# A decoder layer on one core: projections and query features in pieces between the first maxima and around the last results

## The reference

```python
x = layernorm(x + linear_attention(x))        # 16 heads of 64, features relu(q @ RF), relu(k @ RF)
x = layernorm(x + self_and_cross(x, ctx))     # 16 heads of 16: causal self-attention over 512 rows,
                                              # cross-attention over 1024 context rows; the sum goes through Wp + bp
x = layernorm(x + experts(x))                 # 8 experts, 256 -> 1024 -> 256, the best one for each row
```

## Time and profile before

| | us |
|---|---|
| median of 3 runs (2553.83 to 2562.61) | 2555.13 |
| the profiled execution's own time | 2561.64 |
| its span, first to last instruction | 2559.6 |

### The profile page before, as it was taken

How to read it: one execution, slowest core, us unless ns; L and a number is a source line. 1 busy time by engine, 2 the same in 40 slices (tenths; PEclk the granted TensorE clock), 3 DMA queues, 4 the chain that set the end, 5 groups by cost and what they waited for, 6 DMA issues and landing times. The chain is left out here.

```text
span 2559.6 us, 52199 instructions
## 1 busy us (share of the span) xinstructions
PE 2368.7 (93%) x17502; PEld 1508.8 (59%) x17503; DVE 1451.7 (57%) x3670; ACT 997.6 (39%) x1366; POOL 325.6 (13%) x510
## 2 busy tenths in 40 slices
PE   7999989999999999989999999999999999699997
PEld 4566455655565456545664556555654565388887
DVE  2588247833784458625883378347843686234444
ACT  1156313651265116621563146413652166123332
POOL 1000020002000200020000200020002000112222
PEclk9989998999799989999899979997999799899999
DMA  7430025101510061004300250015100610455543
GB/s 219 167 118 22 2 87 186 43 1 59 203 54 2 24 228 63 2 10 163 122 22 4 109 172 32 1 59 214 43 2 27 225 63 2 159 173 167 164 164 116
DMA packets 115129, 236.45 MB, mean 92 GB/s; under 512 B 18078, under 2 KB 42015, under 8 KB 112704
## 3 DMA queue, kind: packets, MB, share of 16 engines
q1 hardware_dynamic: 111472, 224.81, 25.6%
q0 software_dynamic: 3408, 8.41, 0.9%
HBM read 160.92 MB, written 73.17 MB: 91 GB/s over the span
## 5 line engine op out<-in xcount | busy, mean ns | idle before, releaser
L1040 ACT ACTIVATE es<-ps 128x1024 f32<-128x1024 f32 (+1 forms) x704 | 660.1, 983 | 352.3 <-PE ps L686 266.4
L1229 DVE TENSOR_REDUCE craw<-ps 128x1 f32<-128x512 f32 x1024 | 637.7, 684 | 102.9 <-PE ps L651 92.0
L651 PE MATMUL ps<-hk,hq 64*128 64x512 f32 x1024 | 337.8, 528 | 27.5 <-DVE va L1213 17.7
L714 PE MATMUL ps<-es,vca 128*32 128x256 f32 x4096 | 281.2, 386 | 1.1
L651 PEld LDWEIGHTS ps<-hk,hq 64*128 64x128 f32 x1024 | 162.0, 207 | 188.5 <-DVE craw L1229 120.7
L566 POOL TENSOR_SCALAR_AFFINE_SELECT es<-es 128x256 f32<-128x256 f32 x256 | 100.0, 409 | 1215.4 <-ACT es L1040 1215.4
L1226 DVE TENSOR_REDUCE craw<-ps 128x1 f32<-128x512 f32 (+3 forms) x512 | 220.0, 485 | 60.4 <-PE ps L647 57.5
L684 PE MATMUL ps<-hq,hk 64*128 64x512 f32 x1024 | 240.9, 434 | 1.9 <-ACT es L1040 1.9
L686 PE MATMUL ps<-mrow,minus 64*128 64x512 f32 x1024 | 222.7, 400 | 0.0
L714 PEld LDWEIGHTS ps<-es,vca 128*32 128x32 f32 x4096 | 106.6, 109 | 111.7 <-issue 63.9
L1529 ACT ACTIVATE hT<-ph,b1s 128x128 f32<-128x128 f32 x312 | 89.2, 369 | 199.5 <-PE ph L1492 199.5
(11 more groups left out here) (197 smaller groups left out, 2951.2 us busy)
## 6 DMA issues: line engine op xcount, KB each, us to landing
w1s<-in_w1T SPq DMA_DIRECT2D x39, 1024.0 KB, 5.3
hk<-scr_kc SPq DMA_DIRECT2D x64, 512.0 KB, 5.1
scr_kc<-staged SPq DMA_DIRECT2D x16, 1024.0 KB, 3.8
scr_qc<-staged SPq DMA_DIRECT2D x32, 512.0 KB, 4.6
scr_q<-staged SPq DMA_DIRECT2D x32, 512.0 KB, 5.6
hq<-scr_qc SPq DMA_DIRECT2D x64, 256.0 KB, 4.8
hq<-scr_q SPq DMA_DIRECT2D x64, 256.0 KB, 4.3
hk<-scr_k SPq DMA_DIRECT2D x64, 256.0 KB, 5.2
```

The lines of the kernel that those rows point to most:

```text
L651: last = mm(pb, hq[i][at, T + t * P:T + (t + 1) * P], hk[i][at, T + half * BANK:T + (half + 1) * BANK], start=True, stop=True)
L714: last = mm(z[row:row + ZW, (2 - len(tiles)) * P:2 * P], (va if own else vca)[:, j, p * HB + a, :], weights, start=n in (0, NSELF), stop=n ...
L1040: nc.scalar.activation(es[:, k % ERING, :].rearrange("p (a c) -> p a c", a=HB)[:, :, 0:w], eslot[k % 2][:].rearrange("p (a c) -> p a c", a ...
L1229: last = v.reduce_max(craw[p % 2][:, t, a:a + 1, half], pb, AX.X)
```

## The change

- Each job names its PSUM buffer and the jobs that had it before (`SLOT`, `FORMER`), and two small jobs may share one in halves (`HALF`).
- In the first pair, behind each of five groups of three maxima, stands one piece of PE work: k1, then the halves of qf0 and qf1 (of the next batch). qf2 is cut around the last turn of results, qf3 and kf2 around the jobs at the end.
- phi_q has memory of its own; `va` and `vca` have 17 columns per head instead of 32.
- The low parts of qc1, q1 and k1 are made by POOL, from a second copy (`whole`) that ACT writes.
- The value biases are folded into bp at the start ((bv + bcv) Wp), so that ACT copies vc0, vc1 and v; kf0 and kf1 are copied by ACT too.
- Of the sums over phi_k, only the first stays on POOL; the other two are on DVE, behind the routing.
- The next x is loaded after g1, the next context after kc1. The first expert's weights are loaded at the end of the batches, and `experts` loads its rows before b2.

```diff
-VW = 2 * XD + 1
+VW = XD + 1
+JOBS = [
+    ("g0", "A", 0, ("rank",)), ("ksum", "D", 1, ("kf2",)), ("norm", "D", 2, ("gate",)), ("g1", "A", 3, ("kf3",)),
...
+    ("kc1", "B", 0, ("attn0",)), ("x1T", "A", 1, ("attn1",)), ("qc0", "B", 2, ("vc0",)), ("q0", "B", 3, ("vc1",)),
+    ("k0", "B", 0, ("kc1",)), ("v", "A", 2, ("qc0",)), ("qc1", "A", 3, ("q0",)), ("q1", "A", 3, ("q0",)),
+    ("k1", "A", 2, ("v",)), ("qf0", "A", 3, ("qc1", "q1")), ("qf1", "A", 2, ("k1",)),
+    ("qf2", "A", 2, ()), ("yT", "A", 3, ()), ("proj0", "D", 0, ()), ("proj1", "D", 0, ()), ("qf3", "A", 1, ()),
+    ("kf0", "A", 2, ("qf2",)), ("kf1", "A", 3, ("yT",)), ("x2T", "A", 0, ("proj0", "proj1")), ("gate", "D", 2, ("kf0",)),
+    ("kf2", "A", 1, ("qf3",)), ("rank", "D", 0, ("x2T",)), ("kf3", "A", 3, ("kf1",))]
...
+POOL_LOW = ("qc1", "q1", "k1")
+FIRST_PARTS = [("k1", 0), ("qf0", 0), ("qf0", 1), ("qf1", 0), ("qf1", 1)]
+PARTS = {"qf0": 2, "qf1": 2, "qf2": 2, "qf3": 2, "kf2": 2}
...
-    order = take(MAXES + AHEAD)
+    order = []
+    for name, part in FIRST_PARTS:
+        order += take(3)
+        order.append(("part", name, part))
+    order += take(MAXES + AHEAD - 3 * len(FIRST_PARTS))
...
-    return order + turns
+    return order + [("part", "qf2", 0)] + turns + [("part", "qf2", 1)]
...
+        with nc.sbuf_tensor("whole", [P, len(POOL_LOW), T], F32) as whole:
+            pass
         hk.append(sb("hk4", [P, T + TC_], F32R))
+        with nc.sbuf_tensor("big_c", [P, 4 * LR], F32) as big_c:
+            pass
+        vca = sb("vca", [P, NTC, XH, VW])
+        es = sb("es", [P, ERING, HB * BANK])
+        big_a = sb("big_a", [P, NPAIR * T])
+        with nc.sbuf_tensor("big_b", [P, NT * LR], F32) as big_b:
+            pass
+        staged = sb("staged", [P, 2, 2, 2 * T], F32R)
...
             with sp.Fori(0, nb) as b:
                 store(b, "kc0")
+                sp.wait_ge(s_xb, cur(b, 2, 1))
+                sp.sem_inc(s_pace, 1)
+                sp.wait_ge(s_tile, cur(b, NJ, JN["g1"] + 1))
+                sp.sem_inc(s_pace, 1)
+                load_x(following)
                 stored(b, ("kc0",))
...
                 store(b, "kc1")
+                sp.wait_ge(s_tile, cur(b, NJ, JN["kc1"] + 1))
+                sp.sem_inc(s_pace, 1)
+                load_context(following)
                 for n in ("qc0", "q0", "k0"):
                     store(b, n)
...
+            def part(b, name, n, fill):
+                last = fill(ready(b, name) if n == 0 else ps[SLOT[name]], (n,))
+                if n == PARTS[name] - 1:
+                    last.then_inc(s_tile, 1)
...
+                if k == 0:
+                    pe.wait_ge(s_act, cur(b, N_ACT, ACT_AT["qf1"]))
...
-                            last = mm(z[row:row + ZW, (2 - len(tiles)) * P:2 * P], (va if own else vca)[:, j, p * HB + a, :], weights,
+                            last = mm(z[row:row + VW, (2 - len(tiles)) * P:2 * P], (va if own else vca)[:, j, p * HB + a, :], weights,
...
                 job(b, "yT", turn(y_s))
+                part(b, "qf3", 0, qfeat(3))
                 job(b, "proj0", rows(yT_s, wp_s, (0, 1)), act="yT")
                 job(b, "proj1", rows(yT_s, wp_s, (2, 3)))
-                pe.wait_ge(s_x, (b + 2) * 48)
-                for i in range(NQF):
-                    job(b, f"qf{i}", qfeat(i))
+                part(b, "qf3", 1, qfeat(3))
                 job(b, "kf0", kfeat(0))
+                job(b, "kf1", kfeat(1))
                 pe.wait_ge(s_ln, cur(b, 2, 2))
                 job(b, "x2T", turn(x1))
-                job(b, "kf1", kfeat(1))
+                part(b, "kf2", 0, kfeat(2))
...
                 job(b, "gate", gate, act="x2T")
-                job(b, "kf2", kfeat(2))
+                part(b, "kf2", 1, kfeat(2))
...
+                def whole_part(name, bias_n):
+                    t = full(name)
+                    high_part(name, bias_n, 1, T, last=False)
+                    nc.scalar.activation(whole[:, POOL_LOW.index(name), :], t[:, 0:T], ACT.Identity,
+                                         bias=bias_c[:, bias_n, 1:2]).then_inc(s_act, 1)
...
+                for n, name in enumerate(POOL_LOW):
+                    stg, at, _ = STAGED[name]
+                    pool.wait_ge(s_act, cur(b, N_ACT, ACT_AT[name]))
+                    nc.gpsimd.tensor_tensor(stage[:, stg, 1, at:at + T], whole[:, n, :],
+                                            stage[:, stg, 0, at:at + T].bitcast(F32), ALU.subtract).then_inc(s_low, 1)
...
+            def other_sums(psums):
+                v.tensor_tensor(psum23, phik[:, 2, :], phik[:, 3, :], ALU.add).then_inc(s_psum, 1)
+                dve.wait_ge(s_psum, psums)
+                v.tensor_tensor(psum01, psum01, psum23, ALU.add).then_inc(s_psum, 1)
...
+            sp.wait_ge(s_dve, N_DVE * (nb + 1))
+            sp.wait_ge(s_eid, nb)
+            load_weights(sp, eid, w1s, b1s, w1T, b1p, s_w, 0, 0)
...
-            load_weights(0, 0)
             sp.wait_ge(s_moved, B * NT * 16)
             load_rows(0, 0)
+            sp.dma_start(b2s[:], b2.rearrange("e c -> (e c)").unsqueeze(0).broadcast_to([P, E * C])).then_inc(s_w2, 16)
```

More of the change, by code:

```diff
@@ L728, in qfeat, with fill @@
             def qfeat(i):
-                def fill(t):
-                    for a in range(2):
+                def fill(t, halves=(0, 1)):
+                    for a in halves:
                         j = 2 * i + a
@@ L739, in kfeat, with fill @@
             def kfeat(i):
-                def fill(t):
-                    for half in range(2):
+                def fill(t, halves=(0, 1)):
+                    for half in halves:
                         for c in range(KC):
@@ L747, in kfeat @@
                 return fill
-            pe.wait_ge(s_x, 48)
+            pe.wait_ge(s_x, 32)
             pe.wait_ge(s_setup, 3)
-            for i in range(NQF):
-                qfeat(i)(ps[JN[f"qf{i}"] % 4]).then_inc(s_tile, 1)
-            assert JN["kf0"] - JN["qf0"] == 4 and JN["kf1"] - JN["qf2"] == 4
-            assert JN["kf2"] - JN["kf0"] == 4 and JN["kf3"] - JN["kf1"] == 4
-            pe.wait_ge(s_act, ACT_AT["qf0"])
-            kfeat(0)(ps[JN["kf0"] % 4]).then_inc(s_tile, 1)
-            pe.wait_ge(s_tile, JN["kf0"] + 1)
-            pe.sem_inc(s_tile, 1)
-            pe.wait_ge(s_act, ACT_AT["qf2"])
-            kfeat(1)(ps[JN["kf1"] % 4]).then_inc(s_tile, 1)
-            pe.wait_ge(s_tile, JN["kf1"] + 1)
-            pe.sem_inc(s_tile, 1)
-            pe.wait_ge(s_dve, DVE_AT["kf0"])
-            kfeat(2)(ps[JN["kf2"] % 4]).then_inc(s_tile, 1)
-            pe.wait_ge(s_tile, JN["kf2"] + 1)
-            pe.sem_inc(s_tile, 1)
-            pe.wait_ge(s_dve, DVE_AT["kf1"])
-            kfeat(3)(ps[JN["kf3"] % 4]).then_inc(s_tile, 1)
+            for n in range(2 * NQF):
+                if n >= NQF:
+                    pe.wait_ge(s_relu, n - NQF + 1)
+                (qfeat(n) if n < NQF else kfeat(n - NQF))(ps[n % NQF]).then_inc(s_early, 1)
             pe.wait_ge(s_const, 16 * LOADS)
             pe.wait_ge(s_setup, 4)
+            pe.wait_ge(s_relu, NQF + 1)
+            pe.wait_ge(s_fold, 1)
+            for c in range(KC):
+                last = mm(ps[0][:, 0:C], bv_c[:, 0, c:c + 1].broadcast_to([P, P]), wp_s[:, c, :], start=c == 0, stop=c == KC - 1)
+            last.then_inc(s_early, 1)
+            pe.wait_ge(s_early, 2 * NQF + 1)
+            pe.sem_inc(s_tile, NJ)
             with pe.Fori(0, nb) as b:
@@ L1018, in _ @@
                                          ACT.Copy).then_inc(s_act, 1)
+                for k in range(2):
+                    t = full(f"vc{k}")
+                    nc.scalar.activation(vca[:, 4 * k:4 * k + 4, :, 0:XD], t[:].rearrange("p (a h d) -> p a h d", a=4, h=XH),
+                                         ACT.Copy).then_inc(s_act, 1)
                 high_part("kc1", 1, 1, TC_)
@@ L1057, in _ @@
                         keep(p)
+                    elif p == "k1":
+                        whole_part("k1", 0)
+                    elif kind == "part" and n == 1:
+                        relu_q(int(p[-1]), full(p)).then_inc(s_act, 1)
                 t = full("yT")
                 nc.scalar.activation(yT_s, t[:].rearrange("p (c t) -> p c t", c=KC), ACT.Copy).then_inc(s_act, 1)
-                for i in range(NQF):
-                    relu_q(i, full(f"qf{i}"))
+                relu_q(3, full("qf3")).then_inc(s_act, 1)
+                for n in LAST_STAGED:
+                    act.wait_ge(s_st[n], cur(b, ST[n], ST[n]))
+                for i in range(2):
+                    relu_k(i, full(f"kf{i}")).then_inc(s_act, 1)
                 t = full("x2T")
@@ L1262, in _ @@
                 layer_norm()
-                for n in LAST_STAGED:
-                    dve.wait_ge(s_st[n], cur(b, ST[n], ST[n]))
-                for i in range(2):
-                    relu_k(i, full(f"kf{i}"))
                 t = full("gate")
@@ L1358, in experts @@
         sb("w2_place", [P, E * NHC * C])
```

(4 more changed lines are left out.)

239 lines of the change are left out of this document (117 added, 122 removed), and 9 rows, old and new, of the table JOBS.

## The result

The changed kernel takes 2428.31 us (median of 4 runs, 2426.45 to 2432.26) against 2554.48 for the kernel before in the same session: a ratio of 0.9502, 95% interval [0.9478, 0.9526]. 2434 was predicted. The profiled execution has a span of 2427.6 us, 132.0 less than before, at a mean clock of 0.965 instead of 0.931.

What follows compares the result with a forecast made beforehand. PE was taken as full in the heads and loose in the tail, g0 to g1 and projections, with DVE limiting the maxima. Terms -100.5, -3, -1, -17.4 sum to -122, scaled to 2434 us; range 2400 to 2500, forecast's own 2420 to 2450.

Steps and rivals of the forecast that it cites:

- Tail, -10.1 a batch: Last weighing to g0: two query features leave, two fill holes, so 43.03 us becomes 32.9.
- The walk over PE's order: Predicted tail sequence of PE's pieces from the last weighing's end, at 1.72 us per half query feature, to g0 at 32.9.
- the 1.2 us for rank: In the tail, PE's predicted wait because rank stands behind onehot, which DVE finishes 2.9 us after the gate.
- g0 to g1, -4.26: Between g0 and g1: moving two phi_k sums to DVE removes the wait and clock dip, 15.53 to 11.27 us.
- Up to the first exponential, -0.4: Projections to first exponential, per batch: first maximum 3.4 us earlier, stage of maxima 3.0 us longer with pieces inserted.
- 17 columns, 0 with -20 as the other end: Narrower weights of 5888 weighing records: between 0 and 20 us saved in all, taken as 0.
- Start -1, experts' gap -17.4: Key copies on ACT start first g0 earlier, -1 us; earlier POOL finish brings the first expert matmul forward, -17.4 us.
- (1): Rival: pieces inserted among the first pair's maxima run at half clock, 90 us back, 2524; chance 0.12.
- (2): Rival: 17-column weights lose side-by-side running in the weighing, 177 us, 2611, slower than before; chance 0.06.
- (3): Rival: narrower loads do shorten the weighing and the clock returns sooner in the heads, -20 us, 2414; chance 0.10.
- (4): Rival: pieces push the maxima by their whole 8.6 us instead of 3.0, 45 us, 2479; chance 0.10.

Runs made afterwards that it cites:

- The experiment beside the gate: Changed kernel, but POOL starts its first sum over the key features only when the gate is done, beside DVE's routing: 2432.57 us, ratio 0.9535.
- the run of four things: Changed kernel plus rank in the gate's bank, half-length pieces, b2 loaded with the first expert's weights, context behind the first loads: 2379.81 us, ratio 0.9295.
- in the experiment: Changed kernel with the four pieces of qf0 and qf1 back in the tail, only k1 among the maxima: 2469.05 us, ratio 0.9666.

## Why the prediction was right, point by point

- **Tail, -10.1 a batch.** Measured -11.25 on the mean, at 31.1 us instead of 33. The walk over PE's order held, piece for piece up to rank, and g0's wait of 2.57 us for the routing stood where it was said. Wrong was the 1.2 us for rank: the 2.9 us from gate to onehot that I took over held 1.4 us in which DVE stood behind POOL's first sum, which now runs earlier (549.08 to 551.48). The experiment beside the gate shows it: there PE waits 1.49 us for rank.
- **g0 to g1, -4.26.** Measured -2.2; the largest miss, 17 instead of 30 us. The duration I carried over, 11.27 us, was that of a batch whose g0 had waited 1.20 us; here it waits 2.57, and the clock falls in g0 itself in all seven batches, and in norm in four. I had put that wait into the tail's sum and not asked what the clock does behind it; why it fell seven times of seven here and two of seven beside the gate is open. And the cause named was not the one at work: with the sums back on POOL nothing waits for them, because g0, held up by its bank, ends after they do.
- **Up to the first exponential, -0.4.** Measured -3.1 + 3.4 = +0.3. The group came out at 2.57 us instead of 2.4: between maxima a piece takes 1.92 us from start to start (628.10 to 630.02) and not 1.72. The first maximum, said to come 12 to 13 us behind the first projection, came after 14.4: the clock fell in the projections in five of eight batches (14.7 to 14.9 us), and at the full clock it was 13.8. It waits for the cross queries, as expected, but the context in front of them is the reason only in batches with projections at the full clock.
- **17 columns, 0 with -20 as the other end.** Measured -14.8 over the heads. The direct part is some 0.5 x 8 = 4 us, the rest is the clock in that stretch (0.96 to 0.97 before, 0.97 to 0.99 after). What the width is worth depends on its surroundings: 0.9% in the kernel before, nothing measurable in the changed one.
- **Start -1, experts' gap -17.4.** Measured -2.3 and -16.9. Of this the move of the sums brought only 1.1 us, as the run with them on POOL shows. PE still waits there, 4.05 us, for b2 by the kernel's order (the profile names no releaser); in the run of four things, with b2 loaded early, the gap is 2.5 us shorter.
- **The rivals.** (1) Half clock in the pieces: out, 1.00 while they run, 0.93 in the whole stage and 0.65 without them. The Trainium skill ("TensorE: Matmul & The Clock Gate", section "A second HAM failure mode: psum-queue depth-cycling") has it that short pauses between groups that cycle through PSUM banks can make the clock swing between its two levels. The trace agrees for the maxima without pieces, at 0.50 to 0.58 before, 0.64 to 0.71 in the experiment and 0.83 behind the last piece; where the pieces run, PE has no pause (12.86 us busy of 12.86). (2) Out: four products of 17 columns still run side by side, at 2.26 us for 32 records. (3) Its 20 us are real in the kernel before, some 4 of them by the loads and the rest by the clock, as it half said, but in the changed kernel nothing of them can be measured. (4) Out: a piece costs 0.64 us of the stage and not 1.72.

That the total was off by only 6 us (10 between the two profiles, 132 for 122) is partly luck: of the gain forecast, 13 us were missing from g0 to g1 and 5 up to the first exponential, and 15 more than forecast came in the heads, 8 in the tail and 4 between g1 and the projections.

What isn't settled is why the clock falls in one batch and not in the next at the same order of work. The falls in g0 go with the length of the wait in front of it, with seven exceptions; and where g0 to g1 ran at 1.00, the heads behind it mostly ran at 0.97. That falls depend on where earlier falls were is a guess from this; no run here isolates a rule. Nor was every part of the change taken out alone: the moved copies of the keys and values, which go with most of the gain up to the first maximum, the next x behind g1 and the first expert's weights in the tail have no run of their own.

## What to carry to other kernels

A piece of matrix work goes best where another engine sets the pace, in pieces that are shorter than the work that the ring of buffers holds for that engine: 1.92 us against 1.89 us of reductions left DVE idle for 0.69 of every 2.57 us, and half the length left it idle for 0.28 of every 3.36. When a buffer is handed on, look at who reads it last: a bank that rank had used put 6 us of routing in front of the next batch's first product. And before a duration is carried over from another stretch, look at the wait in front of it in both places, and allow for either clock behind it: g0 took 7.13 us behind every wait of 1.19 us, and 8.59 to 8.83 us behind most waits of 2.57 us.

## What was not expected of the hardware

- A change of 0.5 us a batch in the weighing moved the clock of a tail that has nothing to do with it (42.8 to 40.33 us), and the time by 0.9%. A ratio of a per cent can come from where the falls land; stretches at an equal granted clock tell what an edit itself costs.
- A DVE instruction of 0.19 us took 2.10 us beside a POOL instruction that had started 0.30 us earlier, and ended with it.
